# Constant bf16 products on TensorE at six places, and two slots of attention 2's fill moved

## The reference, cut to what matters

```
L0: x = LN(x + selfattn(x), causal, 16 heads);  x = LN(x + crossattn(x, ctx), 16 heads);  x = LN(x + W2 gelu(W1 x))
L1: x += selfattn(x), 4 heads;  x += swiglu(x);  x += crossattn(x, ctx), 4 heads;  x += swiglu(x)
L2: xn = rms(x);  z, gamma from xn
    for t in 0..99:  gate = sigmoid(z_t Wgz + h Wgh);  h = (1 - gate) h + gate z_t + gamma_t h
    x += h_seq + crossattn(xn, ctx), 8 heads + 0.1 v;   x += W2 gelu(W1 rms(x))
L3: a = softmax(x ctx^T) ctx;  out = tanh([x, a] W + b) + x
```

## Time and profile before

| | us |
|---|---|
| median of 3 runs | 1553.15 |
| lowest, highest | 1550.27, 1555.27 |
| the profiled execution | 1554.73 |
| its span on the engines | 1553.0 |

### The profile page before, as it was taken

How to read it: one execution, slowest core, us unless ns; L and a number is a source line. 1 busy time by engine, 2 the same in 40 slices (tenths; PEclk the granted TensorE clock), 3 DMA queues, 4 the chain that set the end, 5 groups by cost and what they waited for, 6 DMA issues and landing times.

```text
span 1553.0 us, 28673 instructions
## 1 busy us (share of the span) xinstructions
PE 1471.4 (95%) x12202; PEld 945.5 (61%) x12202; DVE 767.8 (49%) x1591; ACT 654.4 (42%) x1394; POOL 262.8 (17%) x443
## 2 busy tenths in 40 slices
PE   9888899999999999999999999999899999989998
PEld 8555565656655566555667765554566666655576
DVE  1676666766733256211233332324777777752132
ACT  3555555655635333111244432224554444442343
POOL 1433301010000010000022220000245444510000
PEclk9999999999999999999999999999999999999999
DMA  4311000000000020000200000000000000020032
GB/s 162 104 50 40 21 28 2 2 1 2 2 28 1 0 83 1 21 0 0 82 1 1 1 1 27 0 1 7 28 2 2 2 2 2 2 80 0 0 97 61
DMA packets 19562, 36.85 MB, mean 24 GB/s; under 512 B 2058, under 2 KB 17386, under 8 KB 18282
## 3 DMA queue, kind: packets, MB, share of 16 engines
q1 hardware_dynamic: 19434, 35.01, 6.8%
HBM read 33.36 MB, written 1.64 MB: 23 GB/s over the span
## 4 chain that ended last, share of the span: by engine, by line
PE 86%; DVE 7%; ACT 5%; issue 1%; DVEq 0%; ACTq 0%
PE psum L447 39%; PE psum L839 11%; PE psum L497 8%; PE psum L593 6%; PE psum L633 6%; ACT probs L1179 3%; PE psum L589 3%; DVE maxima L1527 2%; PE psum L532 2%; PE psum L944 2%; PE psum L972 1%; PE psum L953 1%; PE psum L937 1%; PE psum L985 1%; PE psum L627 1%
## 5 line engine op out<-in xcount | busy, mean ns | idle before, releaser
L1527 DVE TENSOR_REDUCE maxima<-psum 100x2 f32<-100x722 f32 (+3 forms) x332 | 245.5, 759 | 114.5 <-PE psum L532 93.9
L447 PE MATMUL psum<-x_resid,weights 128*128 128x400 f32 x832 | 293.7, 503 | 3.0 <-ACT probs L1179 1.7
L447 PEld LDWEIGHTS psum<-x_resid,weights 128*128 128x128 f32 x832 | 156.8, 191 | 120.1 <-issue 5.0
L1179 ACT ACTIVATE probs<-psum 128x800 f32<-128x800 f32 (+3 forms) x224 | 168.1, 787 | 100.1 <-PE psum L593 100.1
L839 PE MATMUL psum<-weights 128*128 128x400 f32 x512 | 174.8, 499 | 0.7 <-DVE maxima L1527 0.7
L447 PE MATMUL psum<-weights,ctx_t 128*128 128x256 f32 (+1 forms) x576 | 155.4, 393 | 1.3 <-DVE max_rows L1538 0.7
L839 PEld LDWEIGHTS psum<-weights 128*128 128x128 f32 x512 | 97.2, 190 | 75.1 <-DVE maxima L1527 0.8
L497 PE MATMUL psum<-ctx_t,weights 128*128 128x361 f32 x384 | 136.7, 481 | 2.1 <-DVE weights L1783 0.8
L1101 ACT ACTIVATE weights<-psum 128x400 f32<-128x400 f32 (+2 forms) x80 | 38.0, 476 | 205.4 <-PE psum L447 205.4
L447 PEld LDWEIGHTS psum<-weights,ctx_t 128*128 128x128 f32 (+1 forms) x576 | 99.1, 184 | 41.5 <-issue 9.5
L633 PE MATMUL psum<-probs,values 128*32 128x100 f32 (+5 forms) x3328 | 112.4, 253 | 2.8 <-ACT q_then_o L1101 1.8
(11 more groups left out here) (167 smaller groups left out, 2089.7 us busy)
## 6 DMA issues: line engine op xcount, KB each, us to landing
weights<-in_w SPq DMA_DIRECT2D x2, 3072.0 KB, 10.2
staged<-in_ctx SPq DMA_DIRECT2D x32, 128.0 KB, 2.1
values<-in_ctx SPq DMA_DIRECT2D x32, 128.0 KB, 2.2
weights<-in_w SPq DMA_DIRECT2D x3, 1024.0 KB, 5.1
weights<-in_src SPq DMA_DIRECT2D x1, 2368.0 KB, 13.8
weights<-in_w SPq DMA_DIRECT2D x1, 2048.0 KB, 7.9
weights<-in_tw SPq DMA_DIRECT2D x2, 1024.0 KB, 5.1
staged<-in_ctx SPq DMA_DIRECT2D x16, 105.0 KB, 2.3
```

Source lines behind the costliest of these rows:

```text
L447: i = nc.tensor.matmul(PS[0:rows, bk, 0:n], lhs, rhs, start=k == 0, stop=k == len(terms) - 1)
L1179: nc.scalar.activation(PT[0:kn, k % PROBS_KEPT, :, 0:n], PS[0:kn, bk:bk + 2, 0:n], ACT.Exp).then_inc(act_results, mark("act", f"{t} p{b} { ...
L1527: nc.vector.reduce_max(top, src, AX).then_inc(dve_results, mark("dve", f"{t} m{b} {j}"))
```

## The change

Two parts. The first adds a helper, `pe_keep_warm`, which issues n products of the matrix of ones with itself (bf16, 384 columns) into a bank that is free, and calls it at these places: before each of the three score calls of attention 2's last batch (6 each), at the end of the gates (6), before the second score call of attention 5's first batch (4), and before the variance product of the norm `r2` of group 0, at the end of attention 5 (10). These are 38 products. Nobody reads their result.

The second part changes attention 2's order: the third `F` of every batch moves behind `X`, and `PRE_AT` of `c0` goes from 1 to 3. With that the queries stand in slots 3 and 4, which lie in the second batch of a group.

```diff
 ORDER = {
-    "c0": "T0 T1 T2 n0 P1 n1 R0 R1 V0 R2 R3 T3 V1 T4 R4 R5 T5 F T6 T7 F K0 V2 K1 F X p0",
+    "c0": "T0 T1 T2 n0 P1 n1 R0 R1 V0 R2 R3 T3 V1 T4 R4 R5 T5 F T6 T7 F K0 V2 K1 X F p0",
 }
-PRE_AT = {"s0": 11, "c0": 1, "s1": 4, "c1": 3, "c2": 1}
+PRE_AT = {"s0": 11, "c0": 3, "s1": 4, "c1": 3, "c2": 1}

+        def pe_keep_warm(pe, ring, n):
+            bk = ring.banks[ring.k % len(ring.banks)]
+            if bk in freed:
+                if due(freed[bk]):
+                    pe.wait_ge(producer(freed[bk]), at(freed[bk]))
+            for k in range(n):
+                nc.tensor.matmul(PS[:, bk, 0:3 * P], ONEB[:, :], ONEB[:, :].unsqueeze(1).broadcast_to([P, 3, P]), start=k == 0, stop=k == n - 1)

 def pe_chain(pe, n, g, ring, more=0):
+            if (n, g) == ("r2", 0):
+                pe_keep_warm(pe, wide["c2"], 10)
             pe_var(pe, n, g, ring)

 def pe_attention(pe, t, step):
                         if kind == "R":
+                            if (t, b) == ("c0", B - 1) and n % 2 == 0:
+                                pe_keep_warm(pe, wide[t], 6)
+                            elif (t, b, n) == ("c2", 0, 1):
+                                pe_keep_warm(pe, held, 4)
                             if not ATT[t]["narrow"] or n % 2 == 0:
                                 pe_scores(pe, t, b, n)

 def pe_gates(pe):
                 advance(opening, OPEN_AT[2][g])
+            pe_keep_warm(pe, held, 6)
             for _ in opening:
                 pass
```

## The result

The changed kernel takes 1548.18 us (median of 20 runs, 1545.43 to 1554.14); the kernel before, run beside it, 1553.27 (median of 20, 1550.26 to 1558.22). The ratio is 0.9975, with a 95% interval of 0.9964 to 0.9986: a gain of 0.25%, sure in its sign and smaller than the 0.3% at which I drew the line. The forecast was 1548.2. The means differ by less than the medians, 1549.38 against 1553.33, and the ratio is nearer to theirs. The profiled execution of the changed kernel is one of its long ones, 1552.43 us, so its sections are compared here one by one, and not its total with the total of before.

The account below looks back on a forecast made before the run. TensorE, 86% of the chain, was taken to bound the kernel. -4.0 + 1.05 + 0.1 - 1.68 = -4.5 us, and -0.4 for the other places, from the median 1553.15 gave 1548.2 us, range 1545.0 to 1551.6.

Parts of the forecast that it names:

- The order: Attention 2: moving queries to batches 1, 5, 9 nets -1.34 us per group, -4.0 us for groups 0, 1 and 2.
- 16.1 and 16.75: Attention 2: expected us between first score calls, 16.1 for batches 0, 4, 8 and 16.75 for batches 1, 5, 9.
- the 0.60 wait: Attention 2, batch 4: TensorE's 0.60 us wait behind the turning, for ScalarE to empty the second queries' bank, would go.
- rival C: Batches 1, 5, 9: the wait moves with the queries, each gets 0.67 us; total -2.9, 1550.2 us; chance 0.06.
- cover: VectorE, behind `max_rows`: 0.89 us idle would hide the residual's sum of 0.6 us, leaving 0.3 us.
- The six products ahead of the first call: Attention 2's last batch: no wait there, so six products lie on TensorE's path, +1.05 us (1.0 to 1.2).
- The twelve in the waits: Attention 2's last batch: products ahead of calls 2 and 3 fill waits of 0.93 and 1.03 us, +0.1 (0 to 0.4).
- The clock at the end of attention 2: Last batch of attention 2: with the waits filled, the 3.4 us stretch at clock 0.50 goes, -1.68 us.
- rival A: Attention 2's end: products don't pay, the clock falls anyway or seldom fell; place costs 1.15, total 1550.3 us; chance 0.17.
- The other three places: Gates' end, attention 5's first batch, before `r2`'s mean: products fit the waits, cost 0; one fall in four executions avoided, -0.4.
- rival B: The other three places gain some 1.6 us more, if the clock fell at one in most executions; 1546.6 us; chance 0.14.
- Rival D: Attention 2: batches 0, 4, 8 lose filled time, more clock falls at 1.69 us each; four give 1555.0 us; chance 0.03.

Follow-up runs that it names:

- Order alone: The changed kernel without any of the 38 constant products, only the new tokens and `PRE_AT`: 1548.47 us, ratio 0.9968 to the kernel before.
- the two kernels that otherwise have their waits filled: The changed kernel with products resized and placed in waits read off the timeline, 1544.32 us (0.9940), and the same without the 20 late products, 1547.59 us (0.9970).
- the fastest kernel: The changed kernel without the six before the first call, with products added in true waits of attention 1, attention 2 and feed-forward 1: 1544.32 us, ratio 0.9940.

## Why the prediction was right or wrong

**The order, -4.0 us: right, and every term of it.** 16.09 and 16.76 were measured for 16.1 and 16.75 in every kernel here with the queries later, the 0.60 wait is gone, no wait for `q_then_o` came (rival C), and VectorE kept 0.41 us of cover. Order alone gives 0.9968, 5.0 us, and 4.3 by the medians. What the prediction did not say is that the swap of the tokens is idle once the queries are later.

**The six products ahead of the first call, +1.05: right** (1.08), and pure cost: the clock is full without them.

**The twelve in the waits, +0.1: right** (0.07).

**The clock at the end of attention 2, -1.68: wrong, the one step that failed.** Two things were off. The size: I took what a slow stretch costs in a batch bounded by TensorE, and this one stood where 0.57 us of waiting for exponentials lay anyway, so it cost 0.92. And the chance: I took one execution's fall for a constant of the kernel, and in two other profiled executions without products there was none. The place therefore cost 0.24 us against an execution with the fall and 1.16 against one without, where I had put -0.5; that is rival A's number, 1.15, which I had given 0.17.

**The other three places, 0 in the profile and -0.4 across executions: the waits right, the value open.** 0.53, 0.51 and 0.68 us of wait left for 0.6, 0.5 and 0.7. Their value is the mechanism of rival B. It measured 3.3 us between the two kernels that otherwise have their waits filled, and nothing that the runs can tell in the change.

**The sum.** By sections it is -4.0 + 0.24 to 1.16 = -2.8 to -3.8 us, plus what the late places give; by the medians -5.1, by the means -3.95. That the median came out at 1548.18 for 1548.2 is partly luck: by sections the clock term was off by 0.8 to 1.7 us, and what made up for it is the draw of slow stretches, which scatters single runs over 9 us, or the late places, which the runs can't tell apart from it. The means are the fairer number, and they say that the change is the reordering and little else. Rival D did not come: attention 2 has two slow stretches in the profile, as before.

The rule of the Trainium skill that I weighed ("TensorE: Matmul & The Clock Gate", "Why this matters for your kernels": one long idle gap) fares badly as the only cause: a fall comes behind a gap of 1.03 us in one execution and stays out behind one of 1.88 in another. The section "A second HAM failure mode: psum-queue depth-cycling" of the same page of the Trainium skill, by which short idles between groups suffice, is the nearer one, but the same waits with a fall and without it at the end of attention 2 show that neither gives the yes or no of a single execution. Why it falls here in one execution and there in another stays open. Open, too, is whether the two slow stretches left in attention 5 (1134.6 and 1168.8 us in the fastest kernel) could be filled away; that was not tried.

## What to carry to other kernels

Move work out of the batch with too much of it into one that has a floor set by another engine: the gain can be read to a tenth from a batch that already has the new shape. Constant products on TensorE pay only inside waits that the timeline names, sized to fit; ahead of an instruction that does not wait they cost their full length, and a rule such as "every batch but the last" put five of twelve there. A fall of the clock seen in one execution is a draw: price it where it stands, waits behind it included, and weigh it by the share of executions that have it.

## What was not expected of the hardware

The slow stretches are not tied to the code alone. Three kernels with the same work and the same two waits, 0.9 and 1.0 us, in the last batch of attention 2 had one fall between them; behind feed-forward 1's open wait of 1.88 us the clock fell in eight profiles of ten. Their number per execution, five in one profile and ten in another, goes with the spread of the times, near 1.1 us each in that pair. And 20 products that nobody reads, in waits of 1.16 to 2.41 us, moved a median by 3.3 us in one kernel, and in another by nothing that the runs can tell.
